# Where VectorE writes the sums that nobody reads: into a scratch tile, or back into the PSUM bank they come from

## The chip, the cores and the metric

The kernel runs on one core of a Trainium2 chip. The time is that of one launch on the device, in microseconds, the median of several runs. VectorE is called DVE in the profile, ScalarE ACT, GpSimd POOL, TensorE PE (its weight loads PEld).

## The reference

A one-layer language model over 8 sequences of 1024 tokens, width 512: embedding (a projection of sines and cosines, and a bias row for each token), attention of 16 heads of width 32, and a mixture of 32 experts, 6 for each token. The change is in the attention:

```python
S = jnp.einsum('hid,hjd->hij', K, Q) * SCALE
delta = idx[:, None] - idx[None, :]
decay = jnp.where(delta < 0, 0.0, -delta.astype(jnp.float32) ** ALPHA)
S = jnp.where(delta < 0, -jnp.inf, S) + decay
C = jax.nn.softmax(S, axis=-1)
attn = jnp.einsum('hij,hjd->hid', C, V)
```

Position i looks at the positions j up to i, and every score gets a decay of one for each step of distance. The softmax needs each row's maximum before its exponentials.

## The kernel before

The program has three stages: `embed`, `attend` and `experts`. In `attend`, a step is four heads (HG = 4) of one sequence; 4 steps make a batch, and 8 batches make 32 steps. Each step has 12 slots (N_GROUPS), and in each slot m the engines do this:

- TensorE (`step` in the tensor block, L1424): the transposed scores of slot m, four heads, for the current step (`scores`, L1296), into banks of a ring of six; a dense piece of work if the plan has one (A); the product of the slot before with the values (`attend_group`, L1322); another dense piece (B); then `row_scores` (L1277), the scores of the *next* step, queries along the partitions, four heads into four banks of the same ring (`row_bank`, L673); and a last dense piece (C). Dense pieces are projections, sums, router and shared expert of the batch before. They share one bank, `ps_dense`.
- VectorE (`step`, L1201): it takes dense results, then does `row_maxima` (L989) of the four banks that `row_scores` filled, a division (`divide_heads`, L1010: a reciprocal L1015 and a product L1018), a part of the batch before's tail (`tail_events`, L1184: gate L1149, choice of experts L1081), and more dense results (the value copy `take_values` L983, with the copy in L986; `find_places` L1123, whose first instruction is L1127).
- ScalarE turns scores into exponentials (`soften`, L860, the instruction in L872), and POOL adds them up (`add_probs`, L795, the instruction in L806).

`row_maxima` goes over the four heads of a slot. For each it waits until TensorE has filled the bank and then issues one `tensor_tensor_reduce`: it adds the decay (a tile in SBUF) to the bank's columns, takes the maximum of the sums along the row, and puts it into `row_max`. The instruction also writes all the sums to an output; nothing reads them. On the chip it is two instructions, both with line L994: the reduction proper (CUSTOM_DVE_ANT_0) and a read of the accumulator, which writes the maximum (DVE_READ_ACCUMULATOR2_ANT). A slot's tile has 128, 256, 384 or 512 columns; of the 12 slots, 6 have 512 and two each have the other widths, 384 columns in the mean. There are 32 x 12 x 4 = 1536 maxima in all.

The semaphore `rows_done` counts finished maxima. TensorE waits for it at two places, since the ring has six banks for the eight that a slot uses: ahead of the third head's matmul in `scores` (L1307 waits, L1309 is the matmul), where it needs the first two maxima of the slot before, and at the start of `row_scores` (L1280 waits, L1285 is the matmul), where it needs all of the slot before. `dense_free` counts the dense results that VectorE or ScalarE has taken; TensorE waits for it ahead of every dense piece. The order on each engine is written out in the code by these loops and by the table of dense pieces (L463 to L472).

Of the kernel before, what the change touches and what calls it, by code (L numbers as in the profile page):

```python
# [22 lines left out]
BF16 = mybir.dt.bfloat16  # L23
# [7 lines left out]
P = 128  # L31
# [6 lines left out]
HG = H // G  # L38
# [3 lines left out]
HALF = T // 2  # L42
# [18 lines left out]
def wait_apart(eng, sem, value, passed):  # L61

    wait_from_1(eng, sem, value)
    eng.sem_inc(passed, 1)
# [499 lines left out]
def attend(nc, io, dram):  # L564
    with ExitStack() as ctx:
        def sb(name, shape, dt=F32):
            return ctx.enter_context(nc.sbuf_tensor("a_" + name, shape, dt))
# [27 lines left out]
        attn_t = sb("attn_t", [P, G, T])  # L595
        sum_inv = [sb(f"sum_inv{half}", [P, HALF]) for half in range(2)]
        row_max = sb("row_max", [P, NT, HG, 2])
        unused = sb("unused", [P, HG, HALF], BF16)
        max_cols = sb("max_cols", [P, NT, P], BF16)
        row_shift = [sb(f"row_shift{p}", [P, T], BF16) for p in range(2)]  # L600

# [63 lines left out]
        def row_shape(k):  # L665

            i, c = ROW_TILES[k]
            return i, c, c * HALF, min((i + 1) * P, (c + 1) * HALF) - c * HALF
# [4 lines left out]
        def row_bank(k, h):  # L673
            return ps_ring[(2 * HG * k + HG + h) % RING]
# [299 lines left out]
        def _(dve):  # L974
# [14 lines left out]
            def row_maxima(s, k):  # L989
                i, c, j0, width = row_shape(k)  # L990
                at = T - P - i * P + j0
                for h in range(HG):
                    wait_apart(dve, rows_full, ITEMS * s + HG * k + h + 1, passed)
                    nc.vector.tensor_tensor_reduce(unused[:, h, 0:width], row_bank(k, h)[:, 0:width],  # L994
                                                   decay[:, at:at + width], 1.0, NEG, ALU.add, ALU.max,
                                                   row_max[:, i, h, c:c + 1]).then_inc(rows_done, 1)

# [203 lines left out]
            def step(st):  # L1201
                chains = ()
                if st.t is not None:
                    chains = (Chain(dve, tail_step, (QUARTERS * st.t + st.g) * TAIL_STEPS),)
                for m in range(N_GROUPS):
                    if m == 0:
                        maxima(st.s, 1)
                    if m == HALF_GROUPS and st.rows:
                        maxima(st.s + 1, 0)
                    take_dense(st, m, A, chains)  # L1210
                    take_dense(st, m, B, chains)
                    if st.rows:
                        row_maxima(st.s + 1, m)
                    if m in LATE_DIVIDE and not st.first:
                        divide_heads(st.s - 1, (st.g - 1) % G, 1, LATE_DIVIDE.index(m), st.number("sums", 1))
                    if m in EARLY_DIVIDE:
                        divide_heads(st.s, st.g, 0, EARLY_DIVIDE.index(m), st.number("sums", 0))
                    if st.t is not None:
                        tail_events(st, m, chains[0])
                    take_dense(st, m, C, chains)  # L1220
                if chains:
                    assert chains[0].n == TAIL_STEPS, chains[0].n
# [16 lines left out]
            for n, (kind, half) in enumerate(PROJECTIONS * 2):  # L1239
                if kind == "v":  # L1240
                    take_values(n // N_PROJ, half, n)
                if n >= N_PROJ:
                    for k in range(2):
                        row_maxima(0, 2 * (n - N_PROJ) + k)
# [415 lines left out]
def build(nc, io):  # L1660

    dram = {
        "hidden": nc.dram_tensor("d_hidden", (NB, T, D), F32, kind="Internal").ap(),
        "normed_t": nc.dram_tensor("d_normed_t", (NB, P, DC, T), F32, kind="Internal").ap(),
        "slots": nc.dram_tensor("d_slots", (E, CAP, XROW), F32, kind="Internal").ap(),
    }
    embed(nc, io, dram)
    attend(nc, io, dram)
    experts(nc, io, dram)
# [67 lines left out]
```

## Time and profile before

| | us |
|---|---|
| median of 3 runs | 3865.16 (3862.11 to 3866.61) |
| the profiled execution | 3872.97 |
| its span, first to last instruction | 3871.2 |
| attention and tail, from the first row maximum to the last | 315 to 3249 |
| granted TensorE clock, mean | 0.920 |

In the rows further down, a line names where the instruction stands, the engine, the operation, and output<-input. "Idle" and what stands behind `<-` tell how long the engine stood still before it and which instruction ended that. In a timeline the first number is the start in us from the start of the span, the second the duration in us. An instruction's record can reach into the next one's: what the next has to wait for is seen from the starts.

### The profile page before, as it was taken

Reading aid. Unit: us, or ns where it says so; the run is one execution under the profiler, and the core shown is the slowest. Engines: PE = TensorE matmul, PEld = TensorE weight load, DVE = VectorE, ACT = ScalarE, POOL = GpSimd, SP = SyncE. Lnnn points to the kernel's source line nnn. Section 1 sums busy time; section 2 is a strip of 40 time slices with the busy share of each in tenths; the row PEclk is TensorE's granted clock in tenths of the full one; section 3 lists DMA queues with packets and bytes.
Section 4 is the critical chain, followed back from the end, with each engine's and each line's share of the span. In section 5 each row is a group of like instructions: output and inputs, shape, how many; then the busy total and the mean of one; then the engine's idle time right before and its main releaser. Section 6 shows DMA issues by size and latency. Waiting matters only on the chain. (4 is left out here: it accounts for less than half of the span.)

```text
span 3871.2 us, 62509 instructions
## 1 busy us (share of the span) xinstructions
PE 3245.3 (84%) x20296; PEld 1670.1 (43%) x20296; DVE 2419.5 (63%) x6622; ACT 1112.7 (29%) x2553; POOL 1671.2 (43%) x924
## 2 busy tenths in 40 slices
PE   4647999888888888888888888889888977655998
PEld 2324444444444444444444444444444433334776
DVE  6733565567667665766576657665776577553554
ACT  3751333233223322332233223322332233101111
POOL 5630354445435443544454445444444446322332
PEclk8878999999999999999999999999999988867999
DMA  5664000021111011101010101010101000104996
GB/s 199 244 271 136 1 28 20 28 77 50 68 51 46 14 34 34 34 12 39 29 34 12 40 28 34 12 40 28 34 12 39 28 12 12 55 25 133 259 259 154
DMA packets 123205, 257.87 MB, mean 67 GB/s; under 512 B 38988, under 2 KB 39628, under 8 KB 120192
## 3 DMA queue, kind: packets, MB, share of 16 engines
q1 hardware_dynamic: 78400, 201.42, 15.8%
q0 software_dynamic: 44048, 49.26, 5.0%
q8 instruction: 169, 2.77, 0.3%
q10 hardware_dynamic: 432, 3.15, 0.2%
q14 instruction: 156, 1.28, 0.1%
HBM read 146.71 MB, written 204.26 MB: 91 GB/s over the span
## 5 line engine op out<-in xcount | busy, mean ns | idle before, releaser
L806 POOL TENSOR_TENSOR a_first_probs<-a_first_probs,a_probs 128x2048 f32<-128x2048 f32 (+3 forms) x320 | 1033.5, 3230 | 1594.1 <-ACT a_probs L872 1375.0
L994 DVE CUSTOM_DVE_ANT_0 a_unused<-a_ps_ring,a_decay 128x512 bf16<-128x512 f32 (+3 forms) x1536 | 773.4, 554 | 515.8 <-PE a_ps_ring L1285 510.2
L872 ACT ACTIVATE a_probs<-a_ps_ring 128x512 f32<-128x512 f32 (+3 forms) x1280 | 505.5, 473 | 794.8 <-PE a_ps_ring L1319 600.1
L810 POOL DMA_INDIRECT d_slots<-a_rows,a_place_i x397 | 395.6, 997 | 226.3 <-DVE a_place_i L1147 141.7
L1309 PE MATMUL a_ps_ring<-a_k_t,a_q_t 32*128 32x512 f32 (+3 forms) x3072 | 412.6, 539 | 72.4 <-DVE a_row_max L994 44.0
L1285 PE MATMUL a_ps_ring<-a_q_t,a_k_t 32*128 32x512 f32 (+3 forms) x3072 | 391.3, 542 | 17.5 <-DVE a_row_max L994 12.6
L1383 PE MATMUL a_ps_dense<-a_sd,a_inner_t 128*128 128x512 f32 x256 | 184.5, 860 | 191.3 <-DVE a_gate_up L1127 188.0
L1273 PE MATMUL a_ps_dense<-a_normed_t,a_q_w 128*128 128x512 f32 x512 | 246.0, 625 | 35.1 <-DVE a_max_cols L980 32.5
L872 ACT ACTIVATE a_first_probs<-a_ps_ring 128x512 f32<-128x512 f32 x256 | 135.6, 605 | 475.8 <-PE a_ps_ring L1319 450.9
L1332 PE MATMUL a_ps_heads<-a_probs,a_values 128*32 128x512 f32 (+3 forms) x2560 | 269.9, 495 | 0.0
L1309 PEld LDWEIGHTS a_ps_ring<-a_k_t,a_q_t 32*128 32x128 f32 x3072 | 146.0, 186 | 274.9 <-issue 147.0
L1352 PE MATMUL a_ps_dense<-a_o_w,a_attn_t 128*128 128x512 f32 x512 | 237.9, 608 | 18.3 <-DVE a_values L986 10.5
L1273 PE MATMUL a_ps_dense<-a_normed_t,a_k_w 128*128 128x512 f32 x512 | 238.4, 609 | 15.7 <-DVE a_residual L1025 9.7
L1269 PEld LDWEIGHTS a_ps_dense<-a_v_w,a_normed_t 128*128 128x128 f32 x2048 | 235.1, 193 | 36.5 <-issue 35.5
L1269 PE MATMUL a_ps_dense<-a_v_w,a_normed_t 128*128 128x128 f32 x2048 | 247.3, 279 | 1.7 <-ACT a_k_t L857 0.9
L1015 DVE RECIPROCAL a_sum_inv<-a_sum_inv 128x128 f32<-128x128 f32 x256 | 242.6, 948 | 1.9 <-ACT a_sum_inv L885 1.9
L1285 PEld LDWEIGHTS a_ps_ring<-a_q_t,a_k_t 32*128 32x128 f32 x3072 | 144.8, 187 | 225.2 <-issue 189.6
L1018 DVE TENSOR_TENSOR a_attn_t<-a_attn_t,a_sum_inv 128x128 f32<-128x128 f32 x256 | 221.8, 866 | 14.3 <-DVE a_sum_inv L1015 0.9
L1008 DVE CAST a_row_shift<-a_ps_dense 128x512 bf16<-128x512 f32 x64 | 44.3, 692 | 238.0 <-PE a_ps_dense L1292 238.0
L1651 POOL DMA_INDIRECT out<-x_y,x_index x64 | 90.2, 1409 | 236.1 <-DMA out<-x_y,x_index 151.9
L1383 PEld LDWEIGHTS a_ps_dense<-a_sd,a_inner_t 128*128 128x128 f32 x256 | 59.8, 259 | 272.7 <-DVE a_inner_t L1162 158.3
L1273 PEld LDWEIGHTS a_ps_dense<-a_normed_t,a_q_w 128*128 128x128 f32 x512 | 95.7, 197 | 160.2 <-issue 152.8
(177 smaller groups left out, 4402.2 us busy)
## 6 DMA issues: line engine op xcount, KB each, us to landing
d_hidden<-e_hidden SPq DMA_DIRECT2D x8, 2048.0 KB, 7.9
d_normed_t<-e_normed_t SPq DMA_DIRECT2D x8, 2048.0 KB, 11.6
a_normed_t<-d_normed_t SPq DMA_DIRECT2D x8, 2048.0 KB
a_residual<-d_hidden SPq DMA_DIRECT2D x64, 256.0 KB
d_hidden<-a_residual SPq DMA_DIRECT2D x64, 256.0 KB
a_hidden<-d_hidden SPq DMA_DIRECT2D x64, 256.0 KB
out<-a_hidden SPq DMA_DIRECT2D x64, 256.0 KB
x_w_gate<-w_gate SPq DMA_DIRECT2D x32, 512.0 KB, 6.3
```

The source lines that it names most:

```text
L806: nc.gpsimd.tensor_tensor(total_of, total_of, probs_of(m)[:, :, 0:width], ALU.add).then_inc(added, 1)
L810: nc.gpsimd.indirect_dma_start(slot_rows, bass.IndirectOffsetOnAxis(ap=place_i[p][:, j, choice:choice + 1], axis=0), rows[p][:, j, :], Non ...
L872: nc.scalar.activation(probs_of(m)[:, h, 0:width], score_bank(m, h)[:, 0:width], ACT.Exp).then_inc(exp_done, 1)
L994: nc.vector.tensor_tensor_reduce(unused[:, h, 0:width], row_bank(k, h)[:, 0:width], decay[:, at:at + width], 1.0, NEG, ALU.add, ALU.max, r ...
L1015: nc.vector.reciprocal(sum_inv[half][:, cols], sum_inv[half][:, cols]).then_inc(sums_inverted, 1)
L1269: mm = nc.tensor.matmul(ps_dense[:, t * P:(t + 1) * P], normed_t[:, c, tile * P:(tile + 1) * P], w[:, c, g * P:(g + 1) * P], start=(c == 0 ...
L1273: mm = nc.tensor.matmul(ps_dense[:], w[:, c, g * P:(g + 1) * P], normed_t[:, c, half_cols(half)], start=(c == 0), stop=(c == DC - 1))
L1285: nc.tensor.matmul(row_bank(k, h)[:, 0:width], k_t[g][dims, i * P:(i + 1) * P], q_t[g][dims, j0:j0 + width], start=True, stop=True).then_i ...
L1309: nc.tensor.matmul(score_bank(m, h)[:, 0:width], q_t[st.g][dims, j * P:(j + 1) * P], k_t[st.g][dims, i0:i0 + width], start=True, stop=False)
L1332: mm = nc.tensor.matmul(ps_heads[dims, at], values[g][:, j, dims], probs_of(m)[:, h, 0:width], start=(j == 0), stop=(j == last_j))
L1352: mm = nc.tensor.matmul(ps_dense[:], attn_t[:, g, i * P:(i + 1) * P], o_w[:, g, :], start=(g == 0), stop=(g == G - 1))
L1383: mm = nc.tensor.matmul(ps_dense[:], inner_t[:, m, j * P:(j + 1) * P], sd[:, m, :], start=(m == 0), stop=(m == MC - 1))
```

## The change

The reduction writes its sums into the same columns of the same bank that it reads them from, in fp32. Before, it wrote them as bf16 into `unused`, an SBUF tile of 4 KB in each partition, which is no longer allocated; the tiles allocated after it (`max_cols`, `row_shift`, `residual`, `hidden`, `rows` and those after them) lie 4 KB lower. The instructions of all engines, their order and their waits stay as they are; the lines below L598 move up by one.

```diff
         row_max = sb("row_max", [P, NT, HG, 2])
-        unused = sb("unused", [P, HG, HALF], BF16)
         max_cols = sb("max_cols", [P, NT, P], BF16)
...
                 for h in range(HG):
                     wait_apart(dve, rows_full, ITEMS * s + HG * k + h + 1, passed)
-                    nc.vector.tensor_tensor_reduce(unused[:, h, 0:width], row_bank(k, h)[:, 0:width],
+                    nc.vector.tensor_tensor_reduce(row_bank(k, h)[:, 0:width], row_bank(k, h)[:, 0:width],
                                                    decay[:, at:at + width], 1.0, NEG, ALU.add, ALU.max,
                                                    row_max[:, i, h, c:c + 1]).then_inc(rows_done, 1)
```

## Rows read from the trace of the kernel before

**Rows 1.** Page, part 1: busy us (share of the span), instructions.
```profile
PE 3245.3 (84%) x20296; PEld 1670.1 (43%) x20296; DVE 2419.5 (63%) x6622; ACT 1112.7 (29%) x2553; POOL 1671.2 (43%) x924
```

**Rows 2.** Busy us by engine in one batch: PE, weight loads, DVE, ACT, POOL, clock.
```profile
1390.00:1735.00 345.00, 303.08 (x2022) 146.35 (x2019) 229.30 (x674) 98.45 (x239) 156.47 (x79) 0.95 0.10 32
```

**Rows 3.** Waits of TensorE: who for whom, us in total, times, longest us.
```profile
PE a_ps_dense L1383 <- DVE a_gate_up L1127: 188.0, 32, 6.7
...
PE a_ps_ring L1309 <- DVE a_row_max L994: 44.0, 64, 5.1
...
PE a_ps_dense L1375 <- DVE a_values L986: 29.0, 19, 1.5
...
PE a_ps_ring L1285 <- DVE a_row_max L994: 12.6, 6, 2.8
PE a_ps_dense L1352 <- DVE a_values L986: 10.5, 7, 1.6
...
PE a_ps_dense L1391 <- DVE a_values L986: 6.2, 18, 0.5
```

**Rows 4.** Waits of the weight loads, whole run, same columns.
```profile
PEld a_ps_ring L1309 <- DVE a_row_max L994: 76.6, 67, 5.3
...
PEld a_ps_ring L1285 <- DVE a_row_max L994: 17.5, 10, 3.6
```

**Rows 5.** Groups by line and shape: count, busy us, mean ns, idle before.
```profile
L806 POOL TENSOR_TENSOR a_first_probs<-a_first_probs,a_probs 128x2048 f32<-128x2048 f32 x128 | 581.5, 4543 | 552.6 <-ACT a_probs L872 506.7 <-PE a_ps_heads L1332 45.9
L994 DVE CUSTOM_DVE_ANT_0 a_unused<-a_ps_ring,a_decay 128x512 bf16<-128x512 f32 x768 | 484.9, 687 | 339.0 <-PE a_ps_ring L1285 339.0
...
L1025 DVE TENSOR_TENSOR a_residual<-a_ps_dense,a_residual 128x512 f32<-128x512 f32 x64 | 44.3, 692 | 161.6 <-PE a_ps_dense L1352 161.6
...
L278 DVE BATCH_NORM_STATS2 e_stats<-e_hidden 128x6 f32<-128x512 f32 x64 | 43.5, 680 | 0.0
```

**Rows 6.** VectorE in order of time, a full slot: start us, us, instruction.
```profile
1458.48 0.69 DVE L994 CUSTOM_DVE_ANT_0 a_unused<-a_ps_ring,a_decay 128x512 bf16<-128x512 f32 x1 [5.57 <-PE a_ps_ring L1285]
1459.10 0.08 DVE L994 DVE_READ_ACCUMULATOR2_ANT a_row_max<- 128x1 f32 x1
1459.10 0.69 DVE L994 CUSTOM_DVE_ANT_0 a_unused<-a_ps_ring,a_decay 128x512 bf16<-128x512 f32 x1
...
1460.93 0.95 DVE L1015 RECIPROCAL a_sum_inv<-a_sum_inv 128x128 f32<-128x128 f32 x1
```

**Rows 7.** VectorE in order of time, two other instructions back to back.
```profile
1539.53 0.69 DVE L1166 TENSOR_TENSOR a_hidden<-a_ps_dense,a_hidden 128x512 f32<-128x512 f32 x1
1540.13 0.22 DVE L1003 TENSOR_TENSOR a_max_cols<-a_row_max 128x16 bf16<-128x16 f32 x1
```

**Rows 8.** TensorE in order of time: four matmuls that add onto banks.
```profile
1477.87 0.40 PE L1313 MATMUL a_ps_ring<-a_row_shift,a_key_shift 5*128 5x512 bf16 x4
```

**Rows 9.** All engines in order of time, slots 10 and 11 of one step.
```profile
1523.47 0.56 DVE L994 CUSTOM_DVE_ANT_0 a_unused<-a_ps_ring,a_decay 128x384 bf16<-128x384 f32 x1 [0.73 <-PE a_ps_ring L1285]
...
1524.43 0.08 DVE L994 DVE_READ_ACCUMULATOR2_ANT a_row_max<- 128x1 f32 x1
...
1524.57 0.38 PE L1309 MATMUL a_ps_ring<-a_k_t,a_q_t 32*128 32x128 f32 x2 [0.68 <-DVE a_row_max L994]
...
1526.37 1.49 DVE L1018 TENSOR_TENSOR a_attn_t<-a_attn_t,a_sum_inv 128x128 f32<-128x128 f32 x1
1526.41 1.29 POOL L806 TENSOR_TENSOR a_first_probs<-a_first_probs,a_probs 128x512 f32<-128x512 f32 x1
...
1531.10 0.55 DVE L1127 TENSOR_TENSOR a_gate_up<-a_is_top,a_ps_dense 128x384 f32<-128x384 bf16 x1
...
1531.78 3.49 PE L1383 MATMUL a_ps_dense<-a_sd,a_inner_t 128*128 128x512 f32 x4 [6.34 <-DVE a_gate_up L1127]
```

**Rows 10.** All engines in order of time: POOL's addition beside row maxima.
```profile
912.34 0.69 DVE L994 CUSTOM_DVE_ANT_0 a_unused<-a_ps_ring,a_decay 128x512 bf16<-128x512 f32 x1 [0.71 <-PE a_ps_ring L1285]
912.35 4.53 POOL L806 TENSOR_TENSOR a_first_probs<-a_first_probs,a_probs 128x2048 f32<-128x2048 f32 x1 [1.55 <-ACT a_probs L872]
```

## The prediction

> **What bounds the kernel now.** I read the busy times first, then one batch of them, then TensorE's waits, then single slots in order of time. TensorE is busy for 84% of the span, VectorE for 63% [rows 1]. In a batch of the middle (345 us) TensorE works 303 us and VectorE 229 us [rows 2]. So TensorE carries the time, and VectorE matters only where TensorE stands still for it. The change touches one kind of VectorE instruction, the row maximum of L994. The question is therefore how long one takes, and how often TensorE waits behind some.
>
> The waits behind row maxima show who pays. TensorE waits 64 + 6 times (56.6 us) directly for the accumulator read that ends a maximum [rows 3]; its weight loads, which come first, wait 67 + 10 times (94.1 us) [rows 4]. These are the same events seen on two rows, so I count 77. The wait stands ahead of the third head's matmul, so two maxima lie in front of each. Another 19 + 7 + 18 = 44 waits (45.7 us) are for the value copy L986 [rows 3], which VectorE reaches only after all four maxima of its slot. The largest, 188.0 us in 32 events, is for L1127 [rows 3], taken apart below. So some 77 x 2 + 44 x 4 = 330 of the 1536 maxima stand in front of a TensorE that waits; the other 1206 run under matmuls. This 330 is an estimate from above: a copy that was late for another reason counts too.
>
> **What the change removes and adds.** Nothing is removed or added as an instruction, and no wait changes: each maximum is still a reduction followed by an accumulator read, four per slot. Three things differ.
>
> *The reduction's output goes to the bank it reads.* Of 512 columns it lasts 687 ns [rows 5], but the next starts earlier: starts at 1458.48 and 1459.10 are 0.61 us apart (0.613 us a piece over the four maxima from 1458.48 to the reciprocal at 1460.93) [rows 6]. I call 0.613 us the step and the last 0.08 us of the record the tail. The step is what later maxima and the reciprocal pay. No VectorE instruction of this trace writes a bank, so the new step has to be bounded from rows near it.
> - Source: an addition that reads a bank lasts 692 ns for 512 columns (L1025), statistics of 512 columns that read no bank 680 ns (L278) [rows 5]. A step of a bank reader with no accumulator read, L1166 to L1003, is 0.60 us [rows 7]. So which memory an instruction reads changes the record by 12 ns at most. The next instruction after a bank reader may read only SBUF (the reciprocal) and starts without a gap [rows 6]. That is the nearest evidence for the destination too: VectorE's fixed part does not follow the memory much.
> - Bank bandwidth: four matmuls of 512 columns that add onto four banks are through in 0.40 us [rows 8]. Adding onto a bank means reading and writing every column of it, and one matmul's 512 columns fit in that 0.40 us against the 0.53 us in which VectorE wants the same at one column per 1.04 ns. (The 1.04 ns is the slope between steps. For 384 columns a step is half of 1523.47 to 1524.43 [rows 9], 0.48 us; 0.613 less 0.48, over 128 columns.) Reading and writing the same bank should thus not halve VectorE's rate.
> - Bounds: from below, the step could lose the 0.013 us by which it exceeds L1166's 0.60 us; the extreme would be all of 0.613 less 512 x 1.04 ns = 0.08 us. From above, the reduction might have to be acknowledged before the read may start (+0.08 us, the tail), and the read's own 0.08 us might be added (+0.16 us in all); or the bank might serve only one access at a time (+0.53 us at 512 columns).
>
> I take 0 for the step, since source rows 12 ns apart are nearest. Over 330 maxima the ends are -4 us (0.013), +26 us (0.08) and +53 us (0.16).
>
> The Trainium skill speaks against the change here. Its page "Perfetto Trace Analysis", section "Optimizing Scalar/DVE Operations", puts the access overhead of a VectorE instruction at about 60 ns on SBUF and about 125 ns on PSUM. If that held for the destination, an estimate from that page is 65 ns x 330 = 21 us, a time of 3887 us. The rows above deny it for the source; no row here shows the destination.
>
> *The tail.* TensorE is released by the end of the accumulator read, whose record is 0.08 us and whose output stays in SBUF [rows 6]. A quicker write of the sums cannot release TensorE earlier, since the read's own end comes last; a slower one can hold it, by at most another 0.08 us. I take 0; the upper end is 77 x 0.08 = 6 us.
>
> *SBUF.* The scratch tile's write stream goes, and the tiles after it lie 4 KB lower. The only neighbour to gain would be POOL: its addition of 128x2048 took 4.53 us where row maxima began in the same moment [rows 10], against a mean of 4.543 us for all 128 of them [rows 5]. Beside the maxima it is no slower, so there is nothing to win: 0. With another layout nothing is issued differently: 0.
>
> **The chain at L1127.** In slot 10 VectorE begins the maxima at 1523.47; the second one's read starts at 1524.43 and lets TensorE go on at 1524.57 after 0.68 us. Exponentials and POOL's addition (1526.41, 1.29 us) follow, and VectorE's product L1018, begun at 1526.37, lasts 1.49 us and ends with POOL's addition. From there gate and L1127 (1531.10) run serially, and TensorE resumes at 1531.78 after 6.34 us [rows 9]. So in this chain too only two maxima count, not four: the other two lie under the POOL addition, which ends the product whenever VectorE arrives. These 32 are among the 77 (the direct wait stands in the same slot). If a step grew by 0.08 us, each chain would grow by 0.16 us.
>
> **The sum.** Step 0, tail 0, SBUF 0: no change. The profiled execution took 3872.97 us (span 3871.2 us), 7.8 us above the median of the three timed runs, 3865.16 us; the change adds nothing to either, so the forecast is 3865 us. Its own range, from runs 4.5 us apart and steps off by 0.01 to 0.02 us, is 3858 to 3873. Under 0.2% (7.7 us) a difference cannot be told from none.
>
> **Rivals.**
> - *A, changing the destination drains the pipe.* Reduction and accumulator read now write two memories, alternately. All destinations in this trace are SBUF, so nothing in it forbids that the read waits until the bank has acknowledged: +0.08 us a maximum, 330 times, 26 us: 3891 us; with the read's 0.08 us as well, 3918 us. The place is each wait at L1309 and each copy L986. It decides from a step growth of 0.024 us (7.7 us / 330). Against it: two source memories alternate freely. The skill's rule (page "VectorE: DVE Perf Modes", section "Two Vector instructions with no wait between them") judges an output only against the last output into the same memory, by its start quadrant, so that two memories do not hold each other; by that rule the step stays at 0.613 us and the time at 3865. Chance 0.15.
> - *B, one access at a time.* The bank alternates between read and write and each column costs 1.04 ns more: 0.40 us for the mean 384 columns, x 330 = 132 us at least, since waits now covered would open: 3997 us or more. Against it the adding matmuls [rows 8]. Chance 0.04.
> - *C, the step shrinks.* The bank takes the sums with less delay than SBUF, and the step drops by 0.013 to 0.04 us: -4 to -13 us, 3852 to 3861 us. For it: the step is 0.013 us longer than that of L1166, so there is something to lose. Against it: the accumulator read still follows and that may be the whole 0.013. Chance 0.16, of which 0.03 stays within 0.2%.
> - *D, only the tail grows*, by up to 0.08 us: up to 3871 us, and with chains that follow perhaps 3875. Chance 0.09, 0.05 of it within 0.2%.
>
> **How the numbers follow.** The forecast has 0.56. Same: 0.56 + 0.03 + 0.05 = 0.64. Faster: 0.13 (C). Slower: 0.15 + 0.04 + 0.04 = 0.23. The range 3853 to 3900 us takes in the forecast, D, most of C and the first form of A; left out are A's longer form (0.07), B (0.04) and the far end of C (0.04), some 0.15.
>
> **What would show it.** If I am right, the 512-column reduction still starts every 0.61 us, its mean is within 15 ns of 687, and TensorE's waits for L994, L986 and L1127 keep their sums within a few us. A: the accumulator read starts 0.69 us after its reduction, and the 188.0 us row grows by some 5 us. B: the mean at 512 columns goes to some 1.2 us. C: steps of 0.60 us or less and shorter waits at L1309. D: steps of 0.61 us, but TensorE starts more than 0.14 us after the second read's start (now 1524.43 to 1524.57). The forecast fails most easily in the one thing that no row shows, a VectorE write into a bank that it is reading.

## The result: slower by 0.6%, where no change was forecast

The changed kernel took 3890.57 us in the median of five runs (3886.12 to 3900.81), the one before 3866.61 us (3862.11 to 3873.28) on the same chip: a ratio of 1.0063, with an interval of 1.0042 to 1.0083. That is 24 us; 0.2% was the bound of what can be told from none. The forecast was 3865 us and no change, and it was wrong. The time lies inside the range given and, as it happens, within half a microsecond of rival A's 3891 us. The profiled execution took 3900.81 us (span 3899.0 us, clock 0.915) against 3872.97 us before. It was the slowest of the five, so what its trace shows is rather more than the 24 us.

The page after, part 1, stands against [rows 1]:

```profile
PE 3271.4 (84%) x20296; PEld 1673.9 (43%) x20296; DVE 2438.8 (63%) x6622; ACT 1114.9 (29%) x2553; POOL 1671.4 (43%) x924
```

Each engine has as many instructions as before, and ScalarE and POOL kept their times within 2.2 us. The span grew by 27.8 us and *TensorE's busy time* by 26.1 us (3245.3 to 3271.4), although not one of its instructions was touched. Had TensorE merely waited longer, its busy time would have stayed. This one line says that most of the loss is not in waits.

The groups by shape, after (line, engine, operation, count, busy us, mean ns, idle before), against [rows 5]:

```profile
L805 POOL TENSOR_TENSOR a_first_probs<-a_first_probs,a_probs 128x2048 f32<-128x2048 f32 x128 | 581.0, 4539 | 571.2 <-ACT a_probs L871 475.8 <-PE a_ps_heads L1331 95.5
L993 DVE CUSTOM_DVE_ANT_0 a_ps_ring<-a_ps_ring,a_decay 128x512 f32<-128x512 f32 x768 | 507.7, 723 | 348.6 <-PE a_ps_ring L1284 348.6
...
L993 DVE DVE_READ_ACCUMULATOR2_ANT a_row_max<- 128x1 f32 x1536 | 216.0, 141 | 0.0
```

The reduction's record went from 687 to 723 ns at 512 columns, and the accumulator read from 83 to 141 ns (127.6 to 216.0 us for all 1536). POOL's addition took 4543 ns before and 4539 now. The starts show what the next instruction pays. VectorE in order of time, after, a full slot, against [rows 6]:

```profile
1469.98 0.70 DVE L993 CUSTOM_DVE_ANT_0 a_ps_ring<-a_ps_ring,a_decay 128x512 f32<-128x512 f32 x1 [5.57 <-PE a_ps_ring L1284]
1470.60 0.14 DVE L993 DVE_READ_ACCUMULATOR2_ANT a_row_max<- 128x1 f32 x1
1470.60 0.73 DVE L993 CUSTOM_DVE_ANT_0 a_ps_ring<-a_ps_ring,a_decay 128x512 f32<-128x512 f32 x1
1471.25 0.14 DVE L993 DVE_READ_ACCUMULATOR2_ANT a_row_max<- 128x1 f32 x1
...
1472.55 0.94 DVE L1014 RECIPROCAL a_sum_inv<-a_sum_inv 128x128 f32<-128x128 f32 x1
```

The first step is 0.62 us as before; the second is 0.65 us, and so are the third and fourth. A slot's four maxima take 2.57 us instead of 2.45. Over all full slots the medians are 0.616, 0.649, 0.649 and 0.649 us against 0.616 and three of 0.611, and a slot as a whole has 2.563 us against 2.450: 0.113 us more. Up to the end of the second read it is 1.406 us against 1.310: 0.096 us more for a wait for two maxima.

The waits of TensorE and of its weight loads, after (who for whom, us in total, times, longest us), against [rows 3, 4]:

```profile
PE a_ps_dense L1382 <- DVE a_gate_up L1126: 183.6, 32, 6.3
PE a_ps_ring L1308 <- DVE a_row_max L993: 47.1, 61, 5.1
...
PE a_ps_dense L1374 <- DVE a_values L985: 28.9, 19, 1.5
PE a_ps_ring L1284 <- DVE a_row_max L993: 13.4, 6, 2.9
...
PE a_ps_dense L1351 <- DVE a_values L985: 11.3, 7, 1.7
PE a_ps_dense L1390 <- DVE a_values L985: 7.7, 19, 0.5
```
```profile
PEld a_ps_ring L1308 <- DVE a_row_max L993: 82.2, 67, 5.3
PEld a_ps_ring L1284 <- DVE a_row_max L993: 19.1, 11, 3.8
```

The direct waits of the weight loads grew by 7.2 us over some 77 events (94.1 to 101.3), 0.093 us each, which is about the 0.096 us of the two maxima. The copies' waits grew by 2.2 us (45.7 to 47.9), and the wait for L1126 shrank by 4.4 us. That is some 5 us in all.

Where the rest went is seen in one slot of the second step of a batch. TensorE in order of time, before, then two stretches of it (from and to, us, then the busy us of PE, PEld, DVE, ACT and POOL with their instructions, then the granted clock; the last two numbers are DMA traffic):

```profile
1189.86 0.70 PE L1309 MATMUL a_ps_ring<-a_k_t,a_q_t 32*128 32x512 f32 x2 [0.69 <-DVE a_row_max L994]
...
1191.13 1.07 PE L1341 MATMUL a_ps_dense<-a_first_probs,a_ones 128*32 128x512 f32 x8
1192.02 1.04 PE L1332 MATMUL a_ps_heads<-a_first_probs,a_values 128*32 128x512 f32 x8
```
```profile
1188.00:1191.10 3.10, 2.41 (x16) 0.59 (x10) 2.61 (x9) 0.49 (x2) 0.00 (x0) 1.00 0.01 3
1191.10:1194.60 3.50, 3.50 (x32) 1.17 (x30) 1.77 (x3) 2.60 (x5) 0.59 (x1) 1.00 0.00 0
```

The same place after, in the same two views, here three stretches:

```profile
1199.92 0.70 PE L1308 MATMUL a_ps_ring<-a_k_t,a_q_t 32*128 32x512 f32 x2 [0.79 <-DVE a_row_max L993]
...
1201.19 1.75 PE L1340 MATMUL a_ps_dense<-a_first_probs,a_ones 128*32 128x512 f32 x8
1202.69 1.95 PE L1331 MATMUL a_ps_heads<-a_first_probs,a_values 128*32 128x512 f32 x8
```
```profile
1198.00:1201.50 3.50, 2.71 (x20) 0.75 (x18) 3.04 (x9) 0.79 (x2) 0.00 (x0) 0.99 0.01 2
1201.50:1205.00 3.50, 3.50 (x20) 0.77 (x12) 0.76 (x2) 2.26 (x5) 0.02 (x1) 0.52 0.00 0
1205.00:1210.00 5.00, 5.00 (x46) 2.75 (x44) 3.83 (x12) 0.63 (x2) 4.84 (x2) 1.00 0.00 0
```

The wait is 0.10 us longer (0.69 to 0.79). Behind it TensorE has work without a gap, but it does it at 0.52 of full clock, that is at 1.2 GHz instead of 2.4: the records of the sixteen matmuls add up to 3.70 us instead of 2.11. A wait that grew by 0.10 us goes with a loss of 1.6 us behind it. Whether that wait is what brings the loss about, the experiments have to tell.

I added this up from the trace for the attention stage, from the first to the last slot of scores (us). "Stretches" are the separate times at the low clock, and "busy at low clock" is TensorE's work in them, which takes about twice as long as at 2.4 GHz (1.95 against 1.04 us above). So about half of its growth is lost time:

| kernel | stage | PE busy | PE idle | at low clock | stretches | busy at low clock |
|---|---|---|---|---|---|---|
| before | 2944.4 | 2605.6 | 338.7 | 329.7 | 40 | 186.5 |
| after | 2973.7 | 2635.2 | 338.5 | 383.0 | 48 | 250.8 |

The stage grew by 29.3 us, idle time by nothing, and (250.8 - 186.5) / 2 = 32 us is what the low clock took, by this estimate. The granted clock is a record and the sum agrees with it; that the longer waits *bring* the low clock is the theory to test.

### The profile page after: what moved, and what is told of

It is laid out like the page before. It is cut to its first block and busy times, and to the rows that moved or that the text cites. A ratio compares the mean times of both kernels' runs of the same rounds, so it can differ in the third digit from the quotient of the medians.

```text
span 3899.0 us, 62509 instructions
## 1 busy us (share of the span) xinstructions
PE 3271.4 (84%) x20296; PEld 1673.9 (43%) x20296; DVE 2438.8 (63%) x6622; ACT 1114.9 (29%) x2553; POOL 1671.4 (43%) x924
## 5 line engine op out<-in xcount | busy, mean ns | idle before, releaser
L993 DVE CUSTOM_DVE_ANT_0 a_ps_ring<-a_ps_ring,a_decay 128x512 f32<-128x512 f32 (+3 forms) x1536 | 815.3, 587 | 520.9 <-PE a_ps_ring L1284 516.7
L993 DVE DVE_READ_ACCUMULATOR2_ANT a_row_max<- 128x1 f32 x1536 | 216.0, 141 | 0.0
L1017 DVE TENSOR_TENSOR a_attn_t<-a_attn_t,a_sum_inv 128x128 f32<-128x128 f32 x256 | 205.6, 803 | 14.3 <-DVE a_sum_inv L1014 0.9
```

The costliest lines, as they stand in the source:

```text
L993: nc.vector.tensor_tensor_reduce(row_bank(k, h)[:, 0:width], row_bank(k, h)[:, 0:width], decay[:, at:at + width], 1.0, NEG, ALU.add, ALU.m ...
```

## The experiments

Theories. **Price:** either (S) the accumulator read and its reduction now write different memories, and each switch costs; or it is the bank itself (reading and writing one bank), the type (fp32), or every VectorE write into PSUM. **Size:** either (W) the time that VectorE takes longer is the whole cause, a few us directly and the rest by stretches of low clock that it brings about; or (L) it is the tiles' new places in SBUF, or (M) the writes into the banks that hurt TensorE.

**e1, the reduction alone.** Behind the kernel's own work VectorE alone runs each form of it eight times, in two groups of four. This adds to the kernel and leaves nothing out. (The lines below are shortened: `|` stands for one form after the other.)

```diff
+four(reduce(o16[:, k, 0:w], src[k][:, 0:w], w, k))   # bank -> SBUF, bf16; then fp32
+four(reduce(src[k][:, 0:w], src[k][:, 0:w], w, k))   # bank -> the same bank; then another bank
+four(reduce(o32[:, k, 0:w], s32[:, k, 0:w], w, k))   # SBUF -> SBUF; then SBUF -> bank
+four(tensor_tensor(o32 | src | dst, src, other))     # plain additions, three destinations
```

> The kernel before, and behind it a block in which VectorE alone runs groups of four instructions at 512 and 128 columns, each group twice: the reduction of L994 from a bank into SBUF bf16, into SBUF fp32, into its own bank, into another bank; from SBUF into SBUF and into a bank; then a plain addition without accumulator into SBUF, its own bank, another bank; then the same addition alternating with a one-column instruction whose output is in SBUF. Theory 1, the destination memory: every reduction into a bank has an accumulator read of 0.14 us and steps of 0.65 us at 512 columns (0.616 for the first), own bank or other, source in a bank or in SBUF; both SBUF forms have 0.083 and 0.61. Theory 2, reading and writing one bank: only the form into its own bank shows 0.14 and 0.65. Theory 3, the wider output element: the fp32 SBUF form shows them too. If the cost belongs to the change of memory from one instruction to the next, the plain additions into a bank keep steps of 0.60 us, and the alternating form into a bank is slower per pair than that into SBUF by 0.04 to 0.1 us.

VectorE in order of time, second and third instruction of each form: sums to SBUF in fp32, own bank, another bank, SBUF to SBUF, SBUF to bank; last the plain additions.

```profile
3883.14 0.08 DVE L1683 DVE_READ_ACCUMULATOR2_ANT p_acc<- 128x1 f32 x1
3883.14 0.69 DVE L1683 CUSTOM_DVE_ANT_0 p_o<-p_src,p_other 128x512 f32<-128x512 f32 x1
...
3888.27 0.14 DVE L1683 DVE_READ_ACCUMULATOR2_ANT p_acc<- 128x1 f32 x1
3888.27 0.73 DVE L1683 CUSTOM_DVE_ANT_0 p_src<-p_src,p_other 128x512 f32<-128x512 f32 x1
...
3893.74 0.14 DVE L1683 DVE_READ_ACCUMULATOR2_ANT p_acc<- 128x1 f32 x1
3893.74 0.73 DVE L1683 CUSTOM_DVE_ANT_0 p_dst<-p_src,p_other 128x512 f32<-128x512 f32 x1
...
3904.36 0.14 DVE L1683 DVE_READ_ACCUMULATOR2_ANT p_acc<- 128x1 f32 x1
3904.36 0.73 DVE L1683 CUSTOM_DVE_ANT_0 p_dst<-p_s,p_other 128x512 f32<-128x512 f32 x1
...
3909.22 5.00 DVE L1698 TENSOR_TENSOR p_o<-p_src,p_other 128x512 f32<-128x512 f32 x8
3914.26 5.02 DVE L1699 TENSOR_TENSOR p_src<-p_src,p_other 128x512 f32<-128x512 f32 x8
3919.31 5.02 DVE L1700 TENSOR_TENSOR p_dst<-p_src,p_other 128x512 f32<-128x512 f32 x8
```

The price follows the destination of the sums alone: any bank 0.14 us a read and 0.65 us a step, SBUF 0.08 and 0.61, wherever the source is. It is neither the same bank nor fp32. And it is not the write into PSUM as such: eight plain additions take 5.02 us into either bank and 5.00 into SBUF. An addition followed by a one-column instruction in SBUF takes 0.66 us whether the addition writes SBUF or a bank. Theory 1 holds, theories 2 and 3 fall. The price belongs to the pair of reduction and accumulator read.

**e9, where the maximum goes.** The same program at 384 columns, with sums and maximum each to SBUF or to a bank.

```diff
+four(reduce(o16 | dst[k], src[k][:, 0:w], w, acc[:, k:k + 1] | dst[k][:, 511:512]))
```

> The kernel before, and behind it VectorE alone with groups of four reductions of 384 columns, each group twice, by where sums and maximum go: SBUF and SBUF; bank and SBUF (the change); SBUF and bank; bank and bank. If the accumulator read waits because its own output goes to another memory than the sums, only the two mixed forms show the longer read (0.14 us against 0.083) and the step of 0.515 against 0.478 us. If a read behind sums that went to a bank is always slow, the second and the fourth form show it. If a write to a bank is slow to be acknowledged whoever makes it, the third shows a longer read too.

In order of time, one read and one reduction of each pair: sums to a bank and maximum to SBUF; sums to SBUF and maximum to a bank; both to a bank.

```profile
3880.67 0.14 DVE L1683 DVE_READ_ACCUMULATOR2_ANT p_acc<- 128x1 f32 x1
3880.67 0.60 DVE L1683 CUSTOM_DVE_ANT_0 p_dst<-p_src,p_other 128x384 f32<-128x384 f32 x1
...
3885.08 0.14 DVE L1683 DVE_READ_ACCUMULATOR2_ANT p_dst<- 128x1 f32 x1
3885.08 0.59 DVE L1683 CUSTOM_DVE_ANT_0 p_o<-p_src,p_other 128x384 bf16<-128x384 f32 x1
...
3889.49 0.09 DVE L1683 DVE_READ_ACCUMULATOR2_ANT p_dst<- 128x1 f32 x1
3889.49 0.56 DVE L1683 CUSTOM_DVE_ANT_0 p_dst<-p_src,p_other 128x384 f32<-128x384 f32 x1
```

The price is there in both mixed forms and gone when both write PSUM. Steps are 0.52 us in the mixed forms and 0.48 us in the other two. S is shown: it is the change of memory between a reduction and its accumulator read, either way round.

**e2, the change once more; e3, the change with the scratch tile kept; e4, the kernel before with the tile moved.** They separate the write from the layout. In e4 the tile is allocated 22 lines later, so that the tiles between lie as in the changed kernel.

```diff
 e3:          unused = sb("unused", [P, HG, HALF], BF16)      # stays, unused
 e3: +        nc.vector.tensor_tensor_reduce(row_bank(k, h)[:, 0:width], ...
 e4: -        unused = sb("unused", [P, HG, HALF], BF16)
 e4:          counts = sb("counts", [P, E])
 e4: +        unused = sb("unused", [P, HG, HALF], BF16)
```

> The changed kernel once more, for a second profile of it and a time beside the next two. All theories: 3884 to 3900 us, ratio about 1.006. If the clock makes most of the loss, the profile has again about 3 to 8 more stretches at the lower TensorE clock than the 34 of before between 620 and 3280 us, but not in all the same places; TensorE's busy sum is above 3245 us by about as much as the span is above 3871.

> The changed kernel with the unused scratch tile still allocated, so that every SBUF tile lies where it lay before. Destination theory: as the changed kernel, ratio 1.004 to 1.008. Layout theory (tiles 4 KB lower cost the time): ratio 1.000.

> The kernel before with its scratch tile allocated behind the tile counts, so that the tiles between lie 4 KB lower as in the changed kernel, and the sums still go to SBUF. Destination theory: ratio 0.999 to 1.001. Layout theory: ratio 1.006.

e2: 3894.87 us, ratio 1.0059 [1.0039, 1.0079]. e3: 3893.86 us, 1.0053 [1.0034, 1.0072]. e4: 3869.8 us, 0.9998 [0.9985, 1.0011]. The loss comes with the write, and the layout has no part in it: L falls.

**e5 and e6, half the heads each; e7 and e8, slot 4 alone and all slots but it.** Slot 4 (counted from 0) is the one in which TensorE waits in every step.

```diff
-nc.vector.tensor_tensor_reduce(unused[:, h, 0:width], row_bank(k, h)[:, 0:width],
+into = row_bank(k, h)[:, 0:width] if h < 2 else unused[:, h, 0:width]
+nc.vector.tensor_tensor_reduce(into, row_bank(k, h)[:, 0:width],
```

(h < 2 is e5; e6 has h >= 2, e7 k == 4, e8 k != 4.)

> The sums of heads 0 and 1 go back into their bank, those of heads 2 and 3 to the SBUF scratch as before. Theory W (TensorE's wait for the first two maxima pays, 0.038 us for the second step and 0.058 us for its accumulator read, and where that lengthened wait lets the TensorE clock fall, 1.8 us more): nearly the whole loss, +18 to +26 us, ratio 1.005 to 1.007, slot 5 of the second step of a batch longer by 1.2 to 1.8 us as in the changed kernel. Theory V (VectorE's total work pays, 0.115 us in each slot wherever it falls): about half the loss, +12 us, ratio 1.003.

> The other half: heads 0 and 1 to SBUF, heads 2 and 3 back into their bank. Theory W: the wait for the first two maxima is as before; 0 to +5 us, ratio 1.000 to 1.001, no slot longer by 1 us or more. Theory V: +12 us, ratio 1.003.

> Only the 128 maxima of slot 4 (4 heads, 32 steps) go back into their bank, 1408 go to SBUF. If the loss were waits alone, it would be 0.096 us where TensorE waits behind slot 4, at most 32 x 0.096 = 3 us, ratio 1.0008. If the clock falls behind that wait, once in a middle batch and twice in the last, as in the changed kernel's profile: 6 to 8 times 1.8 us more, +11 to +17 us, ratio 1.003 to 1.0045, though only a twelfth of the instructions is changed.

> The complement: all maxima but those of slot 4 go back into their bank. If the clock behind slot 4's wait is most of the loss: slot 5 of the second step is as before, and +8 to +13 us are left, ratio 1.002 to 1.0035. If the loss goes with the number of instructions: eleven twelfths of it, +22 us, ratio 1.0055.

e5: 1.0006 [0.9997, 1.0016]. e6: 1.0006 [0.9995, 1.0017]. e7: 1.0003 [0.9991, 1.0014]. e8: 1.0037 [1.0023, 1.0052], 3888.7 us. Two halves that cost 0.06% each, which can't be told from nothing, make 0.6% together. In e5 two maxima take 1.406 us as with the whole change, the direct waits ahead of the third head's matmul are nearly as long (80.9 us; 76.6 before, 82.2 after), and yet nothing is lost. So the expectation that charged the wait for two maxima fell, and theory V, half the loss for half the instructions, fell with it. What e5 lacks is the length of the slot: 2.487 us against 2.563. The expectation for e7 fell too: +11 to +17 us were expected, and 1 us came. In e8 the falls in the sixth slot of the second step are gone, as expected, but 17 us of loss are left, just above the 8 to 13 us expected; others have come in their place.

**e13 to e15, the delay without the bank.** The sums stay in SBUF as before; one-column additions, SBUF to SBUF, are put in front of one head's reduction: two ahead of the second head (e13), one there (e14), two ahead of the fourth (e15). They write two spare columns, by which `total_inv` is wider.

```diff
                     wait_apart(dve, rows_full, ITEMS * s + HG * k + h + 1, passed)
+                    for d in range(2 if h == 1 else 0):
+                        nc.vector.tensor_scalar(total_inv[:, 2 + d:3 + d], decay[:, 0:1], 1.0, None, ALU.add)
```

> The kernel before, its sums still in the scratch tile, with two additions of one column (SBUF to SBUF) ahead of the second head's reduction in each of the 384 slots. Each should take about 0.06 us, so TensorE's wait for two maxima and the slot both grow by about 0.12 us, near the 0.096 and 0.115 us of the changed kernel, with no write of VectorE into a bank. Theory W (the longer waits are the whole cause, directly by some 7 us and through the lowered TensorE clock by the rest): 1.004 to 1.008 times the kernel before, granted clock lower by some 0.005, and low stretches in slot 5 of the second step. Rival M (the write into the bank hurts TensorE itself): the waits alone, 0.12 us x 70 = 8 us, 1.002.

> As the one with two additions, but with one: the wait for two maxima and the slot grow by about 0.06 us. Theory W with a steep start, as the two halves of the change suggest: 1.0005 to 1.002. A loss in proportion to the delay: 1.003. Rival M: 1.001.

> The two additions of one column stand ahead of the fourth head's reduction: the slot of VectorE grows by 0.12 us, the wait for the first two maxima does not. Theory W: the waits that end with the whole slot (slot 4 of each step, and the copies) lengthen, those ahead of the third head's matmul in the other slots do not: 1.000 to 1.001, as with only the last heads writing into their banks. If the slot's length is what counts: 1.004 or more.

These kernels in order of the slot (medians over 178 full slots each: from the first reduction to the instruction behind the fourth, and to the end of the second read; the columns behind the ratio are those of the table above; e2 and e3 are the change once more and the change with its tile kept):

| kernel | slot | two maxima | ratio | stage | PE idle | stretches | busy at low clock |
|---|---|---|---|---|---|---|---|
| before | 2.450 | 1.310 | 1 | 2944.4 | 338.7 | 40 | 186.5 |
| e5 | 2.487 | 1.406 | 1.0006 | 2944.0 | 336.9 | 41 | 192.4 |
| e6 | 2.487 | 1.310 | 1.0006 | 2950.3 | 335.8 | 45 | 208.2 |
| e14 | 2.510 | 1.371 | 0.9989 [0.998, 0.9998] | 2943.6 | 338.3 | 41 | 188.1 |
| e8 (not slot 4) | 2.562 | 1.405 | 1.0037 | 2967.3 | 342.6 | 51 | 227.7 |
| after | 2.563 | 1.406 | 1.0063 | 2973.7 | 338.5 | 48 | 250.8 |
| e2 | 2.563 | 1.407 | 1.0059 | 2970.3 | 340.9 | 46 | 234.5 |
| e3 | 2.563 | 1.407 | 1.0053 | 2966.9 | 340.6 | 45 | 228.3 |
| e13 | 2.571 | 1.432 | 1.0036 [1.0022, 1.005] | 2963.6 | 339.9 | 46 | 225.2 |
| e15 | 2.571 | 1.310 | 1.0042 [1.0028, 1.0055] | 2970.7 | 342.8 | 50 | 235.8 |

Two one-column additions a slot, which touch no bank, cost 3888.32 and 3890.11 us against 3871.55: 17 and 19 us, with falls of the clock as after the change. e13 lies just below what W had let expect (1.004 to 1.008) and above M's 1.002; e14 lies below both. That is W, for some 60 to 80% of the loss (1.0036 and 1.0042 against 1.0053 to 1.0063, intervals that overlap). The traces speak against M for the rest. Count TensorE's work at the low clock at half and add it to its other work in the stage: 2512 us before, 2512, 2512 and 2510 us in e2, e3 and after, 2511 and 2510 us in e13 and e15. So the banks' writes make no matmul longer; what differs is how much of the same work is done at the low clock, and there e2 and e3 (234.5 and 228.3 us) lie beside e13 and e15 (225.2 and 235.8). Up to 0.06 us more a slot costs nothing that can be measured, 0.11 to 0.12 us costs 0.4 to 0.6%: nearer to a threshold than to a slope, in this kernel. And e15 corrects my picture once more: its expectation by W, 1.000 to 1.001, fell. The waits ahead of the third head's matmul did not grow (76.6 us before, 76.3 in e15), and the loss is as large as in e13. In these kernels it goes with the length of the whole slot, not with the wait that I had taken for the main one.

A fall in e15, in the second slot of a third step. TensorE in order of time, the same place before and then e15, and two stretches of e15:

```profile
1237.62 3.78 PE L1383 MATMUL a_ps_dense<-a_sd,a_inner_t 128*128 128x512 f32 x4 [6.69 <-DVE a_gate_up L1127]
1241.32 0.64 PE L1332 MATMUL a_ps_heads<-a_probs,a_values 128*32 128x256 f32 x8
...
1248.55 1.01 PE L1309 MATMUL a_ps_ring<-a_k_t,a_q_t 32*128 32x384 f32 x8 [0.49 <-ACT a_first_probs L872]
...
1249.99 1.07 PE L1341 MATMUL a_ps_dense<-a_first_probs,a_ones 128*32 128x512 f32 x8
```
```profile
1242.83 3.77 PE L1385 MATMUL a_ps_dense<-a_sd,a_inner_t 128*128 128x512 f32 x4 [6.43 <-DVE a_gate_up L1129]
1246.54 1.08 PE L1334 MATMUL a_ps_heads<-a_probs,a_values 128*32 128x256 f32 x8
...
1253.38 0.49 PE L1287 MATMUL a_ps_ring<-a_q_t,a_k_t 32*128 32x128 f32 x4 [0.23 <-ACT a_first_probs L872]
1254.36 1.51 PE L1311 MATMUL a_ps_ring<-a_k_t,a_q_t 32*128 32x384 f32 x8 [0.49 <-ACT a_first_probs L872]
...
1256.66 1.78 PE L1343 MATMUL a_ps_dense<-a_first_probs,a_ones 128*32 128x512 f32 x8
```
```profile
1250.00:1254.80 4.80, 4.08 (x38) 1.80 (x40) 3.70 (x20) 2.55 (x5) 0.00 (x0) 0.99 0.31 102
1254.80:1258.20 3.40, 3.40 (x24) 1.07 (x20) 0.00 (x0) 0.87 (x2) 0.00 (x0) 0.51 0.26 87
```

In the kernel before, the same waits of 0.23 and 0.49 us stand here, to the hundredth, and the clock holds. Neither grew; the clock fell all the same, in this slot of six of the eight batches, and the long wait ahead of them was even longer before (6.69 us against 6.43). So a fall cannot be read off the wait next to it. What does differ is the way there: behind the long wait TensorE stayed at the low clock longer in e15 (the product with the values took 1.08 us against 0.64). Which slot gets the fall differs from kernel to kernel: the sixth slot of the second step in e2, e3 and after (7, 5 and 5 times), the second slot of the third step in e15 (6 times), the fourth of the first step in e8 (4 times).

**e10, e11, e12, unused matmuls in the waits.** If the low clock is what costs, work that nobody needs should help where TensorE stands still. e10 is the changed kernel with eight matmuls ahead of the third head's wait in the sixth slot of two of the four steps; e11 the kernel before, and e12 the changed one, with six matmuls of 512 columns into a free bank in the long wait for L1127 (slot 11 in the numbering from 0).

```diff
+if (kind, arg) == ("down", 0) and st.rows:                       # e11, e12
+    pe.wait_ge(rows_done, ITEMS * (st.s + 1) + HG * 10 + 3)
+    for _ in range(6):
+        nc.tensor.matmul(row_bank(11, 0)[:], ident[:], sd[:, 0, :], start=True, stop=True)
```

> The changed kernel; in slot 5 of the second and fourth step of a batch TensorE does eight extra matmuls of 128 columns (into the dense bank, whose content is dead then) before it waits for the row maxima. They compute nothing that is used. Clock theory (the loss is stretches at 1.2 GHz that follow lengthened waits): the granted clock no longer falls in slot 5 of the second step, that slot loses its 1.2 to 1.7 us, and the whole is 8 to 14 us faster than the changed kernel: ratio to before 1.002 to 1.004. If the loss is the wait itself, the extra matmuls change nothing or cost time: ratio 1.006.

> The kernel before; in slot 11 TensorE does six extra matmuls of 512 columns (some 5 us, into a free bank of the ring, results unused) in the 6.3 us in which it otherwise waits for L1127. Clock theory: the stretches at 1.2 GHz that begin in slot 11 (27 of 40 in the attention of before) go, and with them about 1.5 to 2.5 us each: 40 to 65 us faster, ratio 0.983 to 0.990. Otherwise: no change, 1.000, or slower if the extra matmuls delay the real ones.

> The changed kernel with the same extra matmuls in slot 11. Clock theory: as much faster as e11 is, and the distance between the two stays 15 to 25 us, made in other slots: ratio to before 0.988 to 0.996. If the loss of the change sat in slot 11, the two become equal.

e10: 3897.81 us, 1.0072 [1.0059, 1.0085], where 1.002 to 1.004 was expected. The falls in that slot vanished, as expected, but others appeared in the fourth slot of the first step (4) and the second of the third (5), 53 stretches in all: nothing gained. e11: **3823.55 us, 0.9889 [0.9875, 0.9903]**, faster than both kernels. e12: 3842.65 us, 0.9934 [0.992, 0.9947]. A stretch of 345 us of e11, as [rows 2] is one of before at a clock of 0.95:

```profile
700.00:1045.00 345.00, 325.08 (x2202) 159.94 (x2195) 241.60 (x697) 105.47 (x253) 170.26 (x83) 1.00 0.16 58
```

In it the clock is 1.00. The waits for L1127 of about 6 us go with a low clock in nearly every step of before (27 of the 40 stretches of before begin there, one in e11); the busy time at low clock in the stage fell from 186.5 to 95.8 us, and (186.5 - 95.8) / 2 = 45 us is the gain (3867.49 to 3823.55, 44 us). With the change on top (e12) it is 19 us more than e11, and the busy time at low clock is 136.0 us against 95.8: half of that difference is 20 us. So the loss does not sit in that wait, and it is low clock here too.

## Why the prediction was wrong, point by point

- *TensorE carries the time; VectorE matters where TensorE stands still for it.* Half right. It left out that TensorE's clock depends on how it stands still (e11). I read the granted clock (0.920, and 0.95 in the batch [rows 2]) and made nothing of it. No term of the sum held it, and it was the largest part of the result: TensorE's busy time grew by 26.1 us of the span's 27.8, the waits named in the sum by some 5 us.
- **The step that failed first: "I take 0 for the step, since source rows 12 ns apart are nearest."** The second to fourth steps of a slot grew by 0.038 us (0.028 us in the mean of the four), past the 0.024 us from which rival A was to decide. The nearest row was not near: the reciprocal that starts without a gap behind a bank *reader* says nothing of an accumulator read behind a bank *writer*. The price that I looked for in the rows on the source sits in the pair (e1, e9). A plain write into a bank is indeed free within 0.02 us in eight (e1), so the reasoning would hold for another instruction.
- *"I take 0; the upper end is 77 x 0.08 = 6 us"* for the tail. The read grew by 0.058 us (83 to 141 ns). Together with one longer step that is 0.096 us for a direct wait, measured 0.093 us x 77 = 7 us. The 6 us bound was for the tail alone, and it held: 0.058 us x 77 = 4 us.
- *330 maxima stand in front of a waiting TensorE.* By terms of this kind, 0.038 us x 330 = 13 us and the tail's 0.058 us x 77 = 4 us, 17 us. The direct waits of the weight loads and the copies grew by 9 us, and idle time as a whole not at all. The count was indeed from above.
- *Bank bandwidth and one access at a time.* Right: columns cost no more (e1: 5.02 against 5.00 us for eight additions); B is out.
- *SBUF and layout 0.* Right: POOL's addition 4539 against 4543 ns, e4 at 0.9998.
- *The chain at L1127 is pinned by POOL's addition.* The wait for L1127 did not grow by two steps, but shrank by 4.4 us in sum. No experiment here asks why.
- *Rival A.* Its place, the read whose memory is another than the sums', is the right one. Its reason, an acknowledgement by the bank, is not shown, and does not fit e9, where sums in SBUF and a maximum in a bank cost the same. Its price per maximum was put at 0.08 us, and the step took 0.038. That its 3891 us fits the measured 3890.57 is a coincidence: it multiplied twice the price by a count that was too high and knew nothing of the clock. Its own sign (the read starts 0.69 us after its reduction, the L1127 row grows by 5 us) did not show.
- *The rules of the Trainium skill.* The rows show a read of 141 ns behind a reduction that writes PSUM, 83 ns behind one that writes SBUF. By the Trainium skill's rule (page "VectorE: DVE Perf Modes", section "Two Vector instructions with no wait between them") an output is judged only against the last one into the same memory, the accumulator read's output too, and a held instruction starts only when all earlier ones have finished. The trace agrees for the plain pairs of e1 (0.66 us either way). A reduction and its read across two memories are not held in that full sense either (the read starts 0.62 us after the first reduction in both kernels), but they have a smaller price for which the rule has no place, 0.038 us. The 65 ns between the overheads that the Trainium skill gives on the page "Perfetto Trace Analysis", section "Optimizing Scalar/DVE Operations", are near the read's 58 ns; but plain additions do not show them (5.02 - 5.00 us for eight), and a maximum in the bank beside its sums does not pay them either (0.09 us in e9).

## What stays open

How a longer slot of VectorE makes TensorE's clock fall is not settled: neither in which waits it acts, nor why the loss sets in between 0.06 and 0.11 us a slot in this kernel; that the slot's length is what counts rests on the order of the table and not on a mechanism. e10 shows that one place can't be mended alone. Why the ratios of the change (1.0053 to 1.0063) lie above those of the delays (1.0036 and 1.0042) is open too; it may be chance, since the traces show no slower matmul. Putting the maximum into the bank as well, which by e9 would remove the price of the pair, wasn't tried in the kernel: all eight banks are in use, and the maxima are read again much later.

## What to carry to other kernels

Keep the output of a reduction and of its accumulator read in one memory, both SBUF or both PSUM (measured for `tensor_tensor_reduce` alone). Where the granted clock is under 1 and TensorE carries the time, a delay on another engine is not priced by the waits that it lengthens: compare TensorE's busy time before and after, and put the low clock down as a term of its own, with a wide range. And before looking for tenths of microseconds, look at what stands behind the longest waits: six unused matmuls in a wait of 6 us gained 1.1% here, more than the change lost.

## What the chip showed that I had not expected

- An accumulator read whose memory differs from that of its reduction's output takes 141 ns instead of 83, and the next reduction of the same kind starts 0.038 us later; the first of a row does not (0.616 us both). At 384 columns it is the same: steps of 0.515 us against 0.478 (e9).
- 0.12 us more in each of 384 VectorE slots cost 17 to 19 us of launch time with TensorE's idle time up by 1 and 4 us only (338.7, 339.9 and 342.8 us); 0.06 us more cost nothing (0.9989).
